# A selective-scan layer with a quantized matmul: the first and the last chunk get an order and waits of their own

## The reference

```python
x = x + s6(layernorm(x))            # state-space layer
x = x + quantized(layernorm(x))     # row-wise int8 matmul, plus bias

# s6: xp = x @ x_proj_w.T (96 columns: 64 of rank, 16 B, 16 C)
#     delta = softplus(xp[:, :64] @ dt_proj_w.T + dt_proj_b)
#     h[d, n] = exp(delta[d] * A[d, n]) * h[d, n] + delta[d] * B[n] * x[d]   (over time)
#     y[d] = sum_n h[d, n] * C[n] + D[d] * x[d]                              (16 states n)
# quantized: scale = max(|row|) / 127; q = round(row / scale)
#     out = (q @ weight_q.T) * scale * weight_scale + bias
```

## Time and profile before

| what | value |
|---|---|
| median of 3 runs | 2899.43 us (2896.78 to 2899.49) |
| the profiled execution, its own time | 2896.54 us |
| its span in the trace | 2894.8 us |
| PE busy | 2778.9 us (96%) |
| DVE busy | 2802.3 us (97%) |
| ACT busy | 2760.6 us (95%) |
| POOL busy | 2699.5 us (93%) |
| mean busy share of the 16 DMA engines | q1 25.6%, q0 15.2% of their span |
| mean granted clock of TensorE | 0.994 |

### The profile page before, as it was taken

The page is one execution under the profiler, slowest core; times in us unless marked ns, Lnnn a source line. Parts: engine busy times, 40 slices in busy tenths (PEclk is TensorE's granted clock), DMA queues, the critical chain, the costliest instruction groups (busy, mean ns, idle before and its releaser), DMA issues.

```text
span 2894.8 us, 58144 instructions
## 1 busy us (share of the span) xinstructions
PE 2778.9 (96%) x22144; PEld 2458.1 (85%) x22144; DVE 2802.3 (97%) x2882; ACT 2760.6 (95%) x4546; POOL 2699.5 (93%) x1424
## 2 busy tenths in 40 slices
PE   6999999999999999999999999999999999999995
PEld 5888898888888888888888888888888888888884
DVE  5999999999999999999999999999999999999995
ACT  7999999999999999999999999999999999999993
POOL 4999999999999999999999999999989999999995
PEclk9999999999999999999999999999999999999998
DMA  6334444343453343443434443434533444433332
GB/s 216 89 103 94 113 117 112 110 117 87 110 127 103 103 125 82 117 124 105 110 88 118 117 109 112 112 80 118 132 103 103 96 110 117 112 110 87 74 103 44
DMA packets 161912, 312.12 MB, mean 108 GB/s; under 512 B 74017, under 2 KB 74017, under 8 KB 140898
## 3 DMA queue, kind: packets, MB, share of 16 engines
q1 hardware_dynamic: 127842, 241.30, 25.6%
q0 software_dynamic: 33792, 67.11, 15.2%
HBM read 204.31 MB, written 104.07 MB: 107 GB/s over the span
## 4 chain that ended last, share of the span: by engine, by line
PE 63%; DVE 22%; issue 7%; POOL 5%; ACT 2%; DMA 1%; SPq 0%; DVEq 0%; POOLq 0%; ACTq 0%
PE Y L538 21%; DVE A L635 20%; PE PB L519 16%; PE PB L516 12%; POOL A L378 4%; PE Y L534 3%; PE PM L559 3%; PE PQ L609 3%; PE PQ L597 2%; PE PM L576 1%; PE PM L585 1%; PE PM L550 1%; ACT A L419 1%; DVE ST L651 1%; DVE X L642 1%
## 5 line engine op out<-in xcount | busy, mean ns | idle before, releaser
L378 POOL TENSOR_TENSOR A<-A,CB 128x2048 f32<-128x2048 f32 x512 | 2340.7, 4623 | 17.1 <-DVE A L635 4.3
L635 DVE TENSOR_TENSOR_SCAN A<-A,CAR,PB 128x512 f32<-128x512 f32 x1536 | 1856.6, 1263 | 14.4 <-issue 3.6
L419 ACT ACTIVATE A<-DEL,an 128x512 f32<-128x512 f32 x2048 | 1360.7, 712 | 8.0 <-PE Y L538 7.7
L538 PE MATMUL Y<-idf,A 128*128 128x128 f32 x8192 | 1123.2, 273 | 0.0
L432 ACT ACTIVATE DB<-XN,BC 128x512 f32<-128x512 f32 x1536 | 1036.2, 711 | 3.0 <-DVE XN L663 2.3
L519 PE MATMUL PB<-idf,DB 128*128 128x128 f32 x6144 | 946.2, 277 | 56.6 <-DVE A L635 34.5
L538 PEld LDWEIGHTS Y<-idf,A 128*128 128x128 f32 x8192 | 940.4, 141 | 12.5 <-POOL A L378 0.2
L519 PEld LDWEIGHTS PB<-idf,DB 128*128 128x128 f32 x6144 | 702.8, 141 | 278.6 <-DVE A L635 152.4
L635 DVE TENSOR_TENSOR_SCAN A<-A,PB 128x512 f32<-128x512 f32 x512 | 594.1, 1205 | 20.7 <-PE PB L519 8.3
L516 PE MATMUL PB<-DG,XN 128*128 128x128 f32 x4096 | 551.6, 280 | 11.4 <-DVE A L635 8.0
L516 PEld LDWEIGHTS PB<-DG,XN 128*128 128x128 f32 x4096 | 495.8, 192 | 56.5 <-DVE A L635 45.9
(11 more groups left out here) (70 smaller groups left out, 1529.0 us busy)
## 6 DMA issues: line engine op xcount, KB each, us to landing
CB<-c_rows SPq DMA_DIRECT2D x128, 1024.0 KB, 6.1
X<-in_x SPq DMA_DIRECT2D x32, 1024.0 KB, 5.2
out<-bib SPq DMA_DIRECT2D x32, 1024.0 KB, 9.5
DG<-b_diag SPq DMA_DIRECT2D x32, 1024.0 KB, 11.5
out<-X POOLq DMA_DIRECT2D x32, 1024.0 KB, 9.2
out<-C POOLq DMA_DIRECT2D x32, 1024.0 KB, 9.1
b_diag<-DG SPq DMA_DIRECT2D x2, 1024.0 KB, 9.9
b_diag<-BC SPq DMA_DIRECT2D x128, 2.0 KB, 5.7
```

Of the source, the lines that this page charges most:

```text
L378: gp.tensor_tensor(A[s % NA][:, :, :], A[s % NA][:, :, :], CB[:, s % (4 * NG), :].unsqueeze(1).broadcast_to([128, KB, L]), ALU.mult).then_ ...
L419: act.activation(A[s % NA][:, g, :], DEL[k % 2][:, g, :], ACT.Exp, scale=an[:, g, n:n + 1])\
L538: i = pe.matmul(Y[j][:, g * 128:(g + 1) * 128], A[s % NA][:, g, j * 128:(j + 1) * 128], idf[:, :], is_transpose=True, start=False, stop=(n ...
L635: dve.tensor_tensor_scan(A[s % NA][:, g, :], A[s % NA][:, g, :], PB[(4 * s + g) % 2][:, :], init, ALU.mult, ALU.add).then_inc(s_scan, 1)
```

## The change

1. The table `PLACES` is replaced by another. Two tables are new: `FIRST`, used for chunk 0 (for its first pieces, where the table is shorter), and `LAST`, used for chunk 31. `put_bias` now stands more than three chunks ahead.
2. The load of chunk 0 becomes four transfers of 256 KB, each with a semaphore, and `stats` of chunk 0 waits piece by piece. PE does 48 transposes ahead of its first task. `dd` becomes the task `skip`. In chunk 0 `x_p` waits piece by piece, `d_t` waits for `xp_out` and not for `bc_out`. `act_b` waits for `du` piece by piece for the first unit of every chunk.
3. In the last chunk the last unit's multiply by C is cut into four pieces: three on POOL, the fourth on DVE (`last_c`).
4. In the last chunk the second norm is cut: `mean1`, the wait of `square` and `amax` by piece, the power of the variance ahead of that of the maximum, and `step` on DVE. `square` writes to `XN` in place of `C`, so that it waits for PE's last reading of that buffer and not for the landing of the output of chunk 30.
5. In the last chunk `centre` and `magic` are gone; DVE does both (`last_q`, two instructions per piece). The `q_mm` of a piece waits for that piece's `qt_out` alone. The output goes in four transfers of 256 KB, each as soon as its piece is scaled.

The core of the diff. Of the tables only the entries that the prediction uses are shown; whole lines are cut with "...":

```diff
@@ PLACES @@
-        "act_b": (-98, -94, -93, -85, -81, -77, -59, -26, -18, 9, 16, 29, 53, 54, 55, 58, 65, 82, 83, 95, 96,
+        "act_b": (-113, -109, -106, -92, -86, -83, -81, -76, -55, -47, -46, -36, -35, -33, -32, 10, 54, 54,
...
-        "add_x": (1263,),
+        "add_x": (1199,),
...
-        "load": (-1721,),
-        "load_c": (450, 551, 672, 683),
-        "load_g": (529,),
+        "load": (-1136,),
+        "load_c": (712, 949, 1009, 1023),
+        "load_g": (706,),
...
-        "mean1": (1312,),
-        "put_bias": (-1474,),
+        "mean1": (1217,),
+        "put_bias": (-3324,),
...
-        "square": (1181, 1183, 1230, 1249),
+        "square": (1114, 1137, 1145, 1197),
...
-        "weights": (-838,),
+        "weights": (-639,),
...
+FIRST = {
+        "act_b": (-187, -182, -179, -162, -116, -110, -106, -81, -80, -80, -43, -43),
...
+        "bc_out": (-2361,),
...
+        "decay": (-291, -274, -236, -154, -124, -97, -76, -74, -48, -47, -24, -9),
+        "delta": (-2562, -2481, -2235, -2082),
...
+        "load_c": (370, 676, 793, 1039),
+        "load_g": (-988,),
+        "rstd0": (-4351,),
+        "scan": (-489, -466, -414, -354, -84, -72, 7, 34),
+        "skip": (-5630,),
+        "stats0": (-4972, -4779, -4705, -4673),
+        "store_c": (-2990,),
+        "store_g": (-2410,),
+        "tb": (-1035, -823, -720, -683, -377, -311, -146, -66),
+        "th": (189, 210, 216, 236),
...
+        "x_p": (-4181, -4082, -3798, -3561),
+        "x_t": (-4572, -4543, -4325, -4163),
...
+LAST = {
+        "add_c": (4500,),
+        "add_x": (3842,),
+        "amax": (2268,),
+        "ascale": (4351,),
...
+        "gather": (1267, 1363, 1868, 1954),
+        "last_c": (1224,),
+        "last_q": (3042, 3189, 3380, 3678),
...
+        "mean1": (1250,),
...
+        "q_mm": (3671, 4564, 4827, 5022),
+        "q_t": (3270, 3600, 3958, 4410),
...
+        def place(name, i, p):
+            if p == 0 and i < len(FIRST.get(name, ())):
+                return FIRST[name][i]
+            if p == END and name in LAST:
+                return PERIOD * p + LAST[name][i]
+            return PERIOD * p + PLACES[name][i]
...
+        def rows(p):
+            return XN[(p + 1) % 2] if p == END else C
...
-            load(0)
+            for j in range(T):
+                sp.dma_start(X[0][:, j, :], xf[j * 128:(j + 1) * 128, :]).then_inc(s_x0[j], 16)
...
+            def skip(p):
+                if p:
+                    return
+                gp.wait_ge(s_id, 1)
+                gp.wait_ge(s_w, 80)
+                for g in range(KB):
+                    gp.tensor_scalar(dd[:, g, :], idf[:, :], dks[:, g:g + 1], 1.0, ALU.mult, ALU.mult).then_inc(s_dd, 1)
...
             def ascale(p):
...
+                if p == END:
+                    gp.wait_ge(s_as, 4 * p + 1)
+                    gp.tensor_tensor(RO[:, 0, :], PW[:, 0, :], halves[:, 0, :], ALU.pow).then_inc(s_pw, 1)
+                    gp.wait_ge(s_am, p + T)
+                    gp.tensor_tensor(RO[:, 1, :], PW[:, 1, :], halves[:, 1, :], ALU.pow).then_inc(s_as, 1)
+                    gp.wait_ge(s_pw, 1)
...
             def times_c(k, n):
                 s = NS * k + n
+                if s == NS * NCH - 1:
+                    gp.wait_ge(s_cb[s // 4 % NG], 16 * (s // 4 // NG + 1))
+                    for g in range(KB - 1):
+                        gp.wait_ge(s_scan, 4 * s + g + 1)
+                        gp.tensor_tensor(A[s % NA][:, g, :], A[s % NA][:, g, :], CB[:, s % (4 * NG), :],
+                                         ALU.mult).then_inc(s_mg, 1)
+                    return
...
             def add_c(p):
+                if p == END:
+                    gp.wait_ge(s_ax[p % 2], 16 * (p // 2 + 1))
+                    for j in range(T):
+                        gp.wait_ge(s_o, T * p + j + 1)
+                        gp.dma_start(of[p * L + j * 128:p * L + (j + 1) * 128, :], rows(p)[:, j, :], accum_op=ALU.add)\
+                          .then_inc(s_ac[p % 2], 16)
+                    return
...
             def square(p, j):
+                if j == 0 or p == END:
+                    act.wait_ge(s_nm, p + 1 + j)
...
+                    if p == END:
+                        act.wait_ge(s_tb, 4 * NS * p)
+                    elif p >= 1:
                         act.wait_ge(s_ac[(p - 1) % 2], 16 * ((p - 1) // 2 + 1))
...
             pe.wait_ge(s_id, 1)
+            for i in range(48):
+                pe.transpose(PQ[:, 0:128], idf[:, :], idf[:, :])
...
+            def last_c(p):
+                if p == END:
+                    s = NS * NCH - 1
+                    dve.wait_ge(s_scan, 4 * s + 4)
+                    dve.wait_ge(s_cb[s // 4 % NG], 16 * (s // 4 // NG + 1))
+                    dve.tensor_tensor(A[s % NA][:, KB - 1, :], A[s % NA][:, KB - 1, :], CB[:, s % (4 * NG), :],
+                                      ALU.mult).then_inc(s_mg, 1)
+
+            def last_q(p, j):
+                if p == END:
+                    n = T * p + j
+                    dve.wait_ge(s_st, p + 1)
+                    dve.tensor_scalar(rows(p)[:, j, :], X[p % NX][:, j, :], SX[:, 1, j:j + 1], AM[:, 3, j:j + 1],
+                                      ALU.add, ALU.mult).then_inc(s_c, 1)
+                    dve.wait_ge(s_c, n + 1)
+                    dve.tensor_scalar(rows(p)[:, j, :], rows(p)[:, j, :], MAGIC, None, ALU.add).then_inc(s_t, 1)
```

More of the change, by code:

```diff
@@ L27 @@
-        "du": (-289, -216, -167, -106),
-        "gather": (1178, 1203, 1227, 1233),
-        "load": (-1721,),
-        "load_c": (450, 551, 672, 683),
-        "load_g": (529,),
-        "magic": (1523, 1683),
-        "mean1": (1312,),
-        "put_bias": (-1474,),
-        "q_mm": (1873, 1965, 2028, 2069),
-        "q_t": (1767, 1780, 1799, 1864),
-        "qt_out": (1697, 1759, 1839, 1868),
-        "rstd0": (-1257,),
-        "scale_out": (1962, 2023, 2088, 2173),
-        "scales": (1504,),
@@ new lines @@
+        "load_c": (712, 949, 1009, 1023),
+        "load_g": (706,),
+        "magic": (1657, 1719),
+        "mean1": (1217,),
+        "put_bias": (-3324,),
+        "q_mm": (1874, 1960, 2026, 2069),
+        "q_t": (1768, 1790, 1814, 1865),
+        "qt_out": (1717, 1773, 1807, 1829),
+        "rstd0": (-1137,),
+        "scale_out": (1943, 2007, 2103, 2156),
+        "scales": (1478,),
+        "scan": (56, 88, 119, 125, 129, 129, 149, 166, 170, 175, 176, 215, 223, 228, 231, 256, 272, 277, 293,
@@ new lines @@
+LAST = {
[3 more added lines that the diff above has]
+        "ascale": (4351,),
+        "centre": (3211, 3273, 3476, 4061),
+        "gather": (1267, 1363, 1868, 1954),
+        "last_c": (1224,),
+        "last_q": (3042, 3189, 3380, 3678),
+        "magic": (2236, 2302),
+        "mean1": (1250,),
+        "put_bias": (582,),
+        "q_mm": (3671, 4564, 4827, 5022),
+        "q_t": (3270, 3600, 3958, 4410),
+        "qt_out": (2954, 2962, 3030, 3094),
+        "scale_out": (4865, 4919, 5158, 5258),
+        "scales": (3006,),
+        "square": (1015, 1245, 1515, 1777),
+        "step": (5124,),
@@ L147, in build @@
         s_xl = [sem(f"s_xl{i}") for i in range(NX)]
-        s_cst = sem("s_cst")
+        s_x0 = [sem(f"s_x0{j}") for j in range(T)]
         s_id = sem("s_id")
@@ L679, in scale_out @@
                 dve.wait_ge(s_mm, n + 1)
-                dve.scalar_tensor_tensor(C[:, j, :], bank_q(p, j)[:, :], AM[:, 1, j:j + 1], wsb[:, :],
+                dve.scalar_tensor_tensor(rows(p)[:, j, :], bank_q(p, j)[:, :], AM[:, 1, j:j + 1], wsb[:, :],
                                          ALU.mult, ALU.mult).then_inc(s_o, 1)
-            run(stats0=stats, aggr0=lambda p, i: aggr(p), gather=gather, du=du, amax=lambda p, i: amax(p), scale_out=scale_out, scales=lambda p, i: scales(p), weights=lambda p, i: weights(p),
-                scan=scan)
+            run(stats0=stats, aggr0=lambda p, i: aggr(p), gather=gather, du=du, amax=lambda p, i: amax(p),
+                scale_out=scale_out, scales=lambda p, i: scales(p),
+                weights=lambda p, i: weights(p), last_c=lambda p, i: last_c(p), last_q=last_q, scan=scan)
 _INS = ["x", "a_log", "d_skip", "wxp", "wdt", "dt_b", "wq", "ws", "bias"]
```

171 lines of the change are left out of this document (109 added, 62 removed), and 16 rows, old and new, of the table PLACES.

## The result

The changed kernel takes 2889.2 us (median of 9 runs, 2885.55 to 2891.02), the kernel before 2898.63 beside it (9 runs, 2896.78 to 2899.49): a ratio of 0.9968, 95% interval 0.9958 to 0.9978. Faster, as forecast, and inside the range of 2873 to 2890, but by 9.4 us and not by 17.4 (from 2899.43 to 2882). The profiled execution (2888.41 us, span 2886.6) is 8.2 us shorter in span than that of before (2894.8).

| Part | before | after | difference | forecast |
|---|---|---|---|---|
| start to first scan | 36.95 | 35.37 | -1.6 | -1.0 |
| first scan to the first scan of chunk 1 | 86.1 | 88.5 | +2.4 | 0.0 |
| from there to the end of the last scan | 2727.5 | 2730.5 | +3.0 | 0 (-3 to +3) |
| end of the last scan to the first `gather` | 6.6 | 7.7 | +1.1 | 0 |
| first `gather` to the end | 37.7 | 24.6 | -13.1 | -15.0 |

A forecast was written before the change was run, and what follows sets the result against it. VectorE, busy 87.70 of 88 us per middle chunk, bounds the kernel, so only the ends can win: middle 0, head -1.0, tail -15.0, sum -16.0, 2896.54 to 2880.5; stated median 2882, range 2873 to 2890 (8 in 10).

The forecast's parts named there:

- The squares' wait that would have made the kernel slower: Rival, middle chunks: ACT's earlier `square` stalls up to 5.7 us per chunk if `mean1` is late; 2975 us, chance 0.05.
- The 0.8: Head: `x_p` by piece overlaps with `xt_out`, so the `x_t` and `x_p` stretch goes from 7.83 to 7.0 us.
- The cost of the load in four, +0.7: Head: three extra load issues ahead of the weights on SP delay them, +0.7 us (0 to +1.4).
- The head: Start to chunk 1: -1.0 to the first scan, then +1.0, -2.6 and +1.6; in all -1.0 us (-5 to +3).
- +1.0 for the statistics: Head: the fourth `stats` and `aggr` come among the first scans on DVE, costing 1.0 us.
- -2.0 for the diagonals: Head: the diagonals land at 41 to 44, before unit 2 wants them at 46, saving 2.0 us.
- -2.6 for the diagonals: Head: -2.0 for diagonals landing in time, and -0.6 for two waits behind it at a slow PE clock.
- +1.6 (0 to +3.5): Head: C's first load lands near 45, so POOL's first multiply and PE's first `th` come late, costing 1.6 us.
- can only lose: Middle: VectorE is busy 87.70 of 88 us, so a new order wins next to nothing; forecast 0 (-3 to +3).
- Loses 0 as long as `last_c` (0.6 us) is over by 2856.6: Last unit's multiply in pieces: wins 0, as PE reaches the last 16 at 2856.6; `last_c` has 0.7 us.
- The tail: Last chunk: earlier second norm, rounding on DVE and output in quarters shorten the end by 15.0 us (12.5 to 17).
- both of the prediction's cases (-0.8 and -2.4): Head, `x_t` and `x_p`: -0.8 us if PE's clock falls again after the warm-up, -2.4 if it holds.

The follow-up runs named there:

- tail alone: Kernel before with only the last chunk's edits and its table LAST, ties in the old order: 2884.14 us, ratio 0.9952.
- the last run: Kernel before plus last chunk's edits, first chunk's waits, `skip` behind `rstd0`, diagonals' chain ahead of bias writes, `an` and weight casts later, 20 transposes: 2879.25 us, ratio 0.9926.
- its best part alone: Kernel before with only the last chunk's edits and LAST, under the new sort: 2915.74 us, ratio 1.0060.

## Why the prediction was right, and where it was off

**Right by mechanism.** `dd` kept `rstd0` at 11.18 (forecast 11.4). `d_t` gave 0.48 (0.3), `act_b` 0.57 (0.6), and the stretch from the first `x_t` to `xp_out` shrank from 7.83 to 7.01 (0.8); the first scan came 1.6 and not 1.0 earlier. The diagonals landed before they were wanted, C's load fell behind the bias and PE waited for POOL at the first `th`: both as forecast. The squares' wait that would have made the kernel slower did not come: in the four chunks from 477 to 829 ACT never waited for POOL. The squares of the last chunk came at 2863.14, 7 us nearer to the last `gather` than before.

**Right by luck.** The 0.8 was forecast for `x_p` by piece, with 0 for the warm-up. Without the warm-up, pieces and all, the stretch took 7.98, and 8.07, 7.08 and 7.99 in the three later traces with pieces and no warm-up: in one of four it was shorter than before. So the 0.8 of this trace is the warm-up's, and what the pieces win is not shown. The cost of the load in four, +0.7, is not shown either: `rstd0` came at 10.3 to 11.2 in the eight traces with quarters and `dd` ahead of it, at 10.6 to 11.1 in the four with one load.

**The head: +0.84 in place of -1.0**, little more than the scatter of identical heads, but the parts are clear. From the first scan to the ninth it lost 0.35 us where -1.0 was forecast (+1.0 for the statistics, -2.0 for the diagonals), and from there to chunk 1 it lost 2.1 where +1.0 was forecast (-0.6 and +1.6). The larger miss is the -2.6 for the diagonals. It was -0.5: three waits of 2.63 us together (the first of them in the earlier trace rows) became three of 2.11, though the diagonals were there, because PE was at the low level for 17 us, from about 33 to 50. The prediction put 0.6 of those waits down to a slow PE and took them as won, without a reason for the clock to be back by then. In two traces of the old order in which it was at 1.00 by then, the waits there were 0.39 and 0.21 (tail alone) and 0.27 and 0.21 (the last run). The other term is that for C's load, "+1.6 (0 to +3.5)": the mechanism was right and the size low, still inside its bounds. The load was issued at 34.89, earlier than the 36.5 reckoned with, but took 12.39 us behind four bias writes and the diagonals and landed at 47.28 and not at 45; moving this one issue brought chunk 1 forward by 3.0 us, of which 2.8 lie behind the ninth scan.

**The middle: +3.0 in place of 0**, at the bound. 0.12 us per chunk, no single wait; VectorE was 87.50 of 88 busy. That a table change in a middle so full "can only lose" held for this table. What the prediction did not see is that the diff changed the order by a second way, the sort; on the old table it costs 1.0 us per chunk, and the new table, laid for it, shows nothing of this. Had the table been kept and the new sort taken, the change would have been slower: 2915.74 with its best part alone.

**The last unit: +1.1 in place of 0.** "Loses 0 as long as `last_c` (0.6 us) is over by 2856.6." It took 2.30 us while POOL multiplied, and 0.68 where POOL had done (the runs with the old order). The new order also brings POOL to the last unit 2.6 us behind the last scan, where it had been 0.1. With the old order the first `gather` is 6.6 us behind the last scan, as before, and the forecast of 0 holds.

**The tail: -13.1 in place of -15.0**, three terms. The chain from the first `gather` to the first transpose 8.96 (forecast 8.58): `PW` and the powers stand behind the issue of `add_x`, 1.33 us, on POOL. PE and `scale_out` 8.8 (7.8): the clock again, 5 us at the low level behind 7.69 us of idle. This term alone was 7.6 to 9.2 in the twelve traces with this tail, behind the same idle time of 7.7 us: the second eight transposes took 1.90 here, at the low level, and 1.04 in the shortest. From there to the end 6.8 (6.3). The rounding, which the trace of before did not show, took 0.92 us per piece (forecast 0.85, bounds 0.57 to 1.15). An estimate by the Trainium skill (VectorE: DVE Perf Modes, The perf-mode tier table) was 0.35 per operation; measured were 0.55 with two pointers as operands and 0.43 with a constant, so that the rows of the maximum (0.57) were the nearer guide.

**The warm-up**, forecast to win 0 as the clock would fall ahead of `x_t`. In the profiled execution of the changed kernel it did, behind 3.90 us of idle. The stretch from 16 to 20 us, before and after:

```profile
16.00:20.00 4.00, 3.31 (x17) 3.08 (x16) 0.00 (x0) 2.39 (x4) 0.00 (x0) 1.00 1.03 399
16.00:20.00 4.00, 3.92 (x16) 3.16 (x17) 0.00 (x0) 1.82 (x4) 0.00 (x0) 0.58 1.01 415
```

After the change the slow pace of `x_t` stands beside a granted clock of 0.58. Before, it stands beside 1.00, so that the prediction's "`x_t` ran at the lower level" rests on the pace alone. In another trace of the same head the clock did not fall:

```profile
4.49 8.32 PE L614 MATMUL PQ<-idf 128*128 128x128 f32 x48 [4.49 <-POOL idf L391]
15.60 1.53 PE L667 MATMUL Y<-idf,XN 128*128 128x128 f32 x12 [2.79 <-ACT XN L561]
```

That is the run with C's load moved: idle 2.79, 12 transposes in 1.53 us and not 2.82, first scan 2 us earlier. The rule quoted in the prediction, that an idle PE is throttled again (the Trainium skill, TensorE: Matmul & The Clock Gate, What's actually happening), agrees with the one trace, and the other shows PE idle for 2.79 us and still at 2.4 GHz. So both of the prediction's cases (-0.8 and -2.4) occur, and which one comes differs from trace to trace of much the same head: the first scans came at 33.2 and 33.4 in two of the six traces with the warm-up, at 34.9 to 36.5 in the other four. It is not shown that either reaches the end. In the run with C's load moved the diagonals' landing took the 2 us back; between the changed kernel and the one without the warm-up the wait for C's load stands behind the difference.

## What to carry to other kernels

Before a change at the head of a pipeline, find the transfer that the first round waits for and follow its chain back through the queue that issues it; an earlier start that does not pull this chain forward is given back in full (2.6 us won and 5.3 lost), and a wait queued ahead of it, here a bias row's, can cost more than the edits on the engines win (the one run that moved it held other edits too). Where a hand-made order keeps the bounding engine over 99% busy (87.50 to 87.70 of 88 us here), the order of two tasks that are due at once is part of it: check that a rewritten sort leaves every engine's sequence the same. Take the part of a change that stands outside such a middle alone, and measure it on the old order. And before the parts of two single traces are compared, look how far identical parts differ: here 1.5 us in the head.

## What the runs showed of the hardware

- **VectorE's product of two SBUF operands stands still while POOL multiplies.** 128x512 took 0.68 us beside an idle POOL and 2.30 us beside POOL's products of 1.33 us each, 1.23 apart. It was issued in POOL's second (2858.99), was not let in ahead of the third, which began at 2859.4, and ended at 2861.29, 0.55 behind it. In the three other traces in which the two met it took 1.53 to 2.29 us and ended 0.55 behind POOL's third as well. The Trainium skill (SBUF — State Buffer, SBUF: two separate sides) has the pair of ports that the two share as a lock held for a whole instruction, which blocks a VectorE operation with two SBUF inputs; the trace agrees. The quarter on VectorE is still worth having (+0.62 without it).
- **TensorE's clock can stay at 0.50, its 1.2 GHz level, for 17 us under load.** In the changed kernel it fell in the idle time of 3.7 us ahead of the first B products (at about 33 us) and came back at about 50, with PE busy for 2.53, 3.68 and 3.63 us of the three stretches of 4 us between 36 and 48. It fell in that idle time (3.7 to 4.4 us), or within 0.5 us of its end, in every trace but one, and stayed low for 3.4 us in two of them (before, tail alone in the old order) and for 10 to 17 us in the others. In the one trace with 20 transposes, which cut that idle time to 2.2 us, it did not fall.
- **A load of 1 MB in four quarters delays what is queued behind it.** The first instruction that waits for the bias row, twelve transfers later, started at 24.0 to 25.8 in the ten traces with quarters, at 22.5 to 23.5 in the four with one load. The cleanest pair is the last chunk's edits in the old order without and with the waits of the first chunk: 22.8 and 25.3. The weights did not suffer in the same way (`rstd0`, above).
- **The output in quarters.** The issue of an accumulating write on POOL took 0.86 to 1.09 us for 256 KB; those of 1 MB from `C` took 1.33 to 1.39 in the kernel before.
